# A deformable convolution block on one core: the fusion convolution with four products for two rows instead of six, and the bilinear blends made in the gather slots

## The chip, the cores and the metric

The kernel runs on one core of one Trainium2 chip. The metric is the device time of one execution in microseconds (us), the median of three timed runs. One more execution was profiled, and all rows below come from it.

## The reference, cut to what matters

```python
# x: (4, 128, 80, 80) float32; every conv is 3x3, padding 1, 128 channels out (the offsets: 18)
out_normal = conv(x, w_normal)
offset = concatenate([conv(x, w_offx), conv(x, w_offy)])     # 9 taps x (dy, dx) for each pixel
out_x = deform_conv(x, offset, w_dx)                         # bilinear samples at 9 shifted positions,
out_y = deform_conv(x, offset, w_dy)                         # then a product over channels and taps
out = conv(concatenate([out_normal, out_x, out_y]), w_fusion)  # 384 channels in
out = relu(bn(out, bn1)); out = bn(conv(out, w_conv2), bn2)
return relu(out + x)
# sample = (1-ty)(1-tx)*g00 + (1-ty)tx*g01 + ty(1-tx)*g10 + ty*tx*g11
```

## The kernel before, in words

**Tiling.** Channels lie on the 128 partitions. The four images are cut into 40 strips (NS) of 8 rows by 80 columns, 640 pixels; a half is 320 pixels, a tile 128 pixels, so a strip has 5 tiles. A float32 operand is kept as a rounded part (`hi`, float32r) and the rest (`lo`), and each product is three matmuls: hi·hi, hi·lo, lo·hi (`three`, lines 338 to 346). ScalarE (ACT) makes `hi` by a copy, VectorE (DVE) makes `lo` by a subtraction (`low`, line 636).

**Steps.** The program runs 44 steps of nine taps, all written out in order for each engine. At step i four strips are in work: the second convolution ("C") on strip i-4, the fusion convolution ("F") on strip i-2, the normal convolution ("N") and the deformable taps on strip i, and the offset convolution ("O") for strip i+1. `SLICES` gives the groups of F, N, C and O that TensorE (PE) does before the deformable tap k; F has 27 groups of three matmuls for each half. In the first four steps the order is that of `FIRST_SLICES`.

**One tap.** With T = 9i + k: GpSimd (POOL) issues five gathers for a tap, one for each tile, that bring 4 neighbours x 128 channels for 128 pixels into one of 15 slots of `cells` (line 299). ACT scales the upper two neighbours into `mixed` (`upper`), DVE adds the lower two (`sample`, line 677), ACT scales the left half into `samp` (`left`), DVE adds the right half (line 683). PE turns the five tiles (`turn_samples`, line 372), ACT and DVE make `samp_hi` and `samp_lo` from PSUM, and PE multiplies them (`deform_tap`, 12 matmuls into four banks `acc`). A slot is free for the gather 15 later when its `mixed` is done; a gather is also held back by `pace`, which PE counts up.

**Order on the engines.** Each engine works strictly through its own list. In step i, tap k the lists are: DVE `sample(T+2)`, `samples_low(T+1)`, weights, `indices`, then what ends in this tap of F, N and C; ACT `left(T+2)`, `samples_high(T+1)`, weights, `upper(T+3)`, the evacuations of O, F, N, C; PE `turn_samples(T+1)`, the slices, `deform_tap(T)`. At the end of a strip ACT copies the four `acc` halves to `feat` and DVE makes their `lo`. `feat` holds hi and lo of three groups of 128 channels, ten rows of which the first and last come from the neighbour strips (`top_done`, `bot_done`). SyncE (SP) loads x, the weights and the residual and stores the output.

Of the kernel before, what the change touches and what calls it, by code (L numbers as in the profile page):

```python
# [7 lines left out]
F32 = mybir.dt.float32  # L8
# [58 lines left out]
]  # L67
GROUPS = {"O": 3, "F": 27, "N": 9, "C": 9}

FIRST_SLICES = [  # L70
    [("O", 0, 0, 3), ("O", 1, 0, 3)],
    [("F", 0, 0, 7)],
    [("F", 0, 7, 16)],
    [("F", 0, 16, 25)],
    [("F", 0, 25, 27), ("F", 1, 0, 7)],
    [("F", 1, 7, 16)],
    [("F", 1, 16, 25)],
    [("F", 1, 25, 27), ("N", 0, 0, 7)],
    [("N", 0, 7, 9), ("N", 1, 0, 9)],
]  # L80
FIRST_STEPS = 4
WEIGHTS_AT = {1: {7: 2}, 2: {1: 3}}


def done(slices):

    return [[(j, h) for j, h, a, b in s if b == GROUPS[j]] for s in slices]

# [6 lines left out]
class Flags:  # L95


    def __init__(self, i=None):
        mid = i is None
        self.strip = mid or i < NS  # L100
        self.nxt = mid or i + 1 < NS
        self.load = mid or i + 2 < NS
        self.top = mid or 1 <= i < NS
        self.bot = mid or 1 <= i <= NS
        self.fuse = mid or 2 <= i < NS + 2
        self.mtop = mid or 3 <= i < NS + 2
        self.mbot = mid or 3 <= i <= NS + 2
        self.resid = mid or 3 <= i < NS + 3
        self.second = mid or 4 <= i < NS + 4

        first = not mid and i < FIRST_STEPS
        self.slices = FIRST_SLICES if first else SLICES
        self.done = done(self.slices)
        self.turn = 2 if first else 3
        self.weights = {} if mid else WEIGHTS_AT.get(i, {})

# [9 lines left out]
def at_least(eng, sem, value):  # L126

    if isinstance(value, int) and value <= 0:
        return
    eng.wait_ge(sem, value)  # L130


def deform_block(nc, x, xflat, table, weights, bn, const, out):
    ctx = ExitStack()
    with ctx:
# [22 lines left out]
        feat = sb("feat", [128, 2, 6, SLOT_ROWS, PITCH], F32R)  # L158
        mid = sb("mid", [128, 2, 2, SLOT_ROWS, PITCH], F32R)

        late = sb("late", [128, 18 * C])
        resid = late[:, 0:2 * PIX].rearrange("p (a n) -> p a n", n=PIX)
        mid_f = late[:, 2 * PIX:3 * PIX].rearrange("p (a n) -> p a n", n=HALF)
# [12 lines left out]
        mixed = sb("mixed", [128, 2, TILES, 2 * C])  # L176
# [8 lines left out]
        acc = [bank(f"acc{n}") for n in range(4)]  # L185
# [16 lines left out]
        slot_taken = sem("slot_taken")  # L202
# [6 lines left out]
        acc_hi_done, acc_lo_done = sem("acc_hi_done"), sem("acc_lo_done")  # L209
        n_done, n_hi_done, n_lo_done = sem("n_done"), sem("n_hi_done"), sem("n_lo_done")  # L210
        top_done, bot_done = sem("top_done"), sem("bot_done")
        f_done, f_out, mid_hi_done, mid_lo_done = sem("f_done"), sem("f_out"), sem("mid_hi_done"), sem("mid_lo_done")
# [23 lines left out]
        def _(eng):  # L236
            def load_x(c):

                start = c * (ROWS * PITCH) + c // STRIPS * (CELLS - H * PITCH) + (1 + PITCH * (LEAD - 1))

                at_least(eng, x_lo_done, c)
                eng.dma_start(x_raw[:], xflat[:, bass.ds(start, SLOT)]).then_inc(x_in, 16)

            def load_weights(n):
                a, b = CHUNKS[n]
                eng.dma_start(stage(n), weights[:, a:b]).then_inc(w_in[n], 16)
# [5 lines left out]
            load_weights(1)  # L252
            load_x(1)

            def step(i, par, fl):
                if isinstance(i, int) and i == 0:
                    eng.wait_ge(samp_done, PER // 3)
                if fl.load:
                    load_x(i + 2)
                if isinstance(i, int) and i == 1:  # L260
                    eng.wait_ge(w_lo_done, 2)
                    load_weights(2)
                    eng.wait_ge(w_lo_done, 3)
                    load_weights(3)
                if fl.resid:
                    s = i - 3
                    slot = 1 - par
                    if isinstance(i, int) and s == 0:
                        eng.wait_ge(w_lo_done, 4)

                    at_least(eng, out_stored[slot], 16 * (s // 2) if isinstance(s, int) else 8 * (s - slot))
                    eng.dma_start(resid[:, slot], x[:, bass.ds(s * PIX, PIX)]).then_inc(resid_in[slot], 16)
                if fl.second:
                    s = i - 4
                    at_least(eng, out_ready, 2 * s + 2)
                    eng.dma_start(out[:, bass.ds(s * PIX, PIX)], resid[:, par]).then_inc(out_stored[par], 16)
# [9 lines left out]
        def _(eng):  # L286
            eng.memset(feat[:].bitcast(F32), 0.0).then_inc(zeroed, 1)
            eng.memset(mid[:].bitcast(F32), 0.0).then_inc(zeroed, 1)

            def gather(c, par, b):  # L290
                at_least(eng, idx_ready, c + 1)
                for q in range(PER):
                    k, j, g = q // TILES, q % TILES, q % GSLOTS
                    at_least(eng, mixed_done, PER * c + q - GSLOTS + 1)
                    at_least(eng, pace, PER * c + q - PACE_LAG + 1)
                    if not isinstance(c, int):

                        eng.sem_inc(slot_taken, 1)
# [9 lines left out]

# [7 lines left out]
        def _(eng):  # L316
            def wcol(base, n):
                return slice((base + n) * C, (base + n + 1) * C)

            def offsets(par, half):  # L320

                for n in range(9):
                    ky, (w, part) = n // 3, ((0, x_hi), (1, x_hi), (0, x_lo))[n % 3]
                    rows = slice(half * HR + ky, half * HR + ky + HR)
                    ins = eng.matmul(work[half][:, 0:HR * PITCH], w_off[:, ky, w].rearrange("p g n -> p (g n)"),  # L325
# [22 lines left out]
            def conv(job, half, a, b, par):  # L348

                for n in range(a, b):  # L350
                    g, k = n // TAPS, n % TAPS
                    rows = slice(half * HR + k // 3, half * HR + k // 3 + HR)
                    cols = slice(k % 3, k % 3 + W)
                    if job == "F":
                        hi, lo, base = feat[:, par, 2 * g, rows, cols], feat[:, par, 2 * g + 1, rows, cols], FUSE
# [7 lines left out]
                    ins = three(work[half][:, 0:HALF], wcol(base, n), hi, lo, n == 0, n == GROUPS[job] - 1, int(mark))  # L363
                if b == GROUPS[job]:
# [10 lines left out]
            def deform_tap(T, tp, k):  # L375
                at_least(eng, samp_lo_done, T + 1)
                rest = TILES - ticks[0]
                for d, base in enumerate((DEFX, DEFY)):
                    for half in range(2):
                        n = 2 * d + half  # L380
                        px = slice(half * HALF, (half + 1) * HALF)
                        ins = three(acc[n][:, 0:HALF], wcol(base, k), samp_hi[:, tp, px], samp_lo[:, tp, px],
# [10 lines left out]
            eng.wait_ge(w_lo_done, 2)  # L393
# [450 lines left out]
```

## Time and profile before

| | us |
|---|---|
| median of 3 runs (2705.27 to 2708.77) | 2706.47 |
| the profiled execution | 2705.52 |
| its span | 2703.7 |

| engine | busy us | share | instructions |
|---|---|---|---|
| PE | 2606.2 | 96% | 17840 |
| DVE | 1845.7 | 68% | 4940 |
| ACT | 2001.4 | 74% | 4925 |
| POOL | 1881.7 | 70% | 1806 |

The granted TensorE clock was 0.984 over the span. Busy time of PE overlaps from one matmul to the next, so its distance from start to start says more than its mean duration. An engine's busy time leaves out the issue of its next instruction: POOL shows 70%, and between two gathers there is always some idle time. A duration in a timeline row with "x5" is that of five instructions from the first start to the last end. Idle time in square brackets stands before the instruction, with what ended it.

### The profile page before, as it was taken

How to read it: one execution, taken by the hardware profiler on the slowest of the kernel's cores; microseconds unless marked ns; L12 is line 12 of the kernel's file. 1: busy time of each engine (PE TensorE's matmuls, PEld its weight loads, DVE VectorE, ACT ScalarE, POOL GpSimd, SP SyncE). 2: the span in 40 equal slices, each digit the busy share in tenths (PEclk: the TensorE clock that was granted, in tenths of full speed). 3: DMA queues.
4: the chain of work that ended last, by engine and by line, in shares of the span. 5: the costliest groups of instructions: out<-in, count | busy, mean ns of one | idle time of the engine just before them, and what ended most of it. 6: DMA issues, size and time to landing. Idle time of an engine off the chain costs nothing.

```text
span 2703.7 us, 51420 instructions
## 1 busy us (share of the span) xinstructions
PE 2606.2 (96%) x17840; PEld 2598.1 (96%) x17840; DVE 1845.7 (68%) x4940; ACT 2001.4 (74%) x4925; POOL 1881.7 (70%) x1806
## 2 busy tenths in 40 slices
PE   3679999999999999999999999999999999999999
PEld 3679999999999999999999999999999999999999
DVE  5777776766676777777767776776766776777730
ACT  5678787777777777777777777777777777777741
POOL 6777777767777676777777776777767777676720
PEclk7789999999999999999999999999999999999999
DMA  5766766767666676666666666666666666666620
GB/s 170 219 203 198 213 205 205 205 189 209 197 205 199 201 206 205 200 200 204 199 203 200 203 198 201 200 200 197 200 194 206 200 205 200 203 207 195 194 76 20
DMA packets 162404, 522.70 MB, mean 193 GB/s; under 512 B 30944, under 2 KB 31072, under 8 KB 161760
## 3 DMA queue, kind: packets, MB, share of 16 engines
q0 software_dynamic: 144000, 471.97, 59.9%
q1 hardware_dynamic: 18144, 47.44, 5.1%
q8 instruction: 141, 2.31, 0.3%
q14 instruction: 119, 0.97, 0.1%
HBM read 506.18 MB, written 13.11 MB: 192 GB/s over the span
## 4 chain that ended last, share of the span: by engine, by line
PE 91%; DVE 2%; ACT 2%; DMA 2%; issue 1%; POOL 1%; ACTq 0%; POOLq 0%; DVEq 0%
PE work L340 19%; PE work L346 19%; PE work L343 19%; PE acc L343 7%; PE acc L340 7%; PE acc L346 7%; PE turned L372 7%; PE work L325 4%; DMA cells<-in_cells,index 2%; POOL cells L299 1%; DVE mixed L677 1%; ACT mixed L472 1%; PE work L332 1%; ACT samp L472 1%; DVE samp L683 0%
## 5 line engine op out<-in xcount | busy, mean ns | idle before, releaser
L299 POOL DMA_INDIRECT cells<-in_cells,index x1800 | 1870.4, 1039 | 705.1 <-issue 342.2
L472 ACT ACTIVATE mixed<-cells,wgt 128x256 f32<-128x256 f32 x1800 | 761.4, 499 | 51.2 <-DMA cells<-in_cells,index 50.4
L472 ACT ACTIVATE samp<-mixed,wgt 128x128 f32<-128x128 f32 x1800 | 620.5, 395 | 205.8 <-DVE mixed L677 197.2
L677 DVE SCALAR_TENSOR_TENSOR mixed<-cells,wgt,mixed 128x256 f32<-128x256 f32 x1800 | 745.9, 477 | 35.0 <-ACT mixed L472 33.4
L340 PE MATMUL work<-feat,w_hi 128*128 128x320 f32 x2160 | 691.4, 320 | 1.4 <-ACT off_c L471 1.4
L346 PE MATMUL work<-feat,w_lo 128*128 128x320 f32 x2160 | 676.0, 313 | 0.0
L343 PE MATMUL work<-feat,w_hi 128*128 128x320 f32 x2160 | 675.7, 313 | 0.0
L683 DVE SCALAR_TENSOR_TENSOR samp<-mixed,wgt,samp 128x128 f32<-128x128 f32 x1800 | 512.5, 345 | 59.5 <-ACT samp L472 59.5
L636 DVE TENSOR_TENSOR samp_lo<-turned,samp_hi 128x640 fp32r<-128x640 f32 x360 | 294.5, 818 | 273.8 <-ACT samp_hi L471 273.8
L340 PE MATMUL acc<-samp_hi,w_hi 128*128 128x320 f32 x1440 | 448.8, 312 | 0.0
L343 PE MATMUL acc<-samp_lo,w_hi 128*128 128x320 f32 x1440 | 447.6, 311 | 0.0
L346 PE MATMUL acc<-samp_hi,w_lo 128*128 128x320 f32 x1440 | 447.5, 311 | 0.0
L471 ACT ACTIVATE samp_hi<-turned 128x640 fp32r<-128x640 f32 x360 | 249.8, 694 | 248.2 <-PE turned L372 247.1
L340 PEld LDWEIGHTS work<-feat,w_hi 128*128 128x128 f32 x2160 | 408.4, 189 | 1.9 <-issue 1.9
L343 PEld LDWEIGHTS work<-feat,w_hi 128*128 128x128 f32 x2160 | 408.5, 189 | 0.0
L346 PEld LDWEIGHTS work<-feat,w_lo 128*128 128x128 f32 x2160 | 408.1, 189 | 0.0
L372 PE MATMUL turned<-cst,samp 128*128 128x128 f32 x1800 | 260.7, 276 | 70.0 <-DVE samp_lo L636 49.1
L372 PEld LDWEIGHTS turned<-cst,samp 128*128 128x128 f32 x1800 | 221.4, 143 | 76.0 <-issue 49.0
L340 PEld LDWEIGHTS acc<-samp_hi,w_hi 128*128 128x128 f32 x1440 | 273.9, 190 | 0.0
L343 PEld LDWEIGHTS acc<-samp_lo,w_hi 128*128 128x128 f32 x1440 | 273.3, 190 | 0.0
L346 PEld LDWEIGHTS acc<-samp_hi,w_lo 128*128 128x128 f32 x1440 | 273.1, 190 | 0.0
L340 PE MATMUL work<-mid,w_hi 128*128 128x320 f32 x720 | 230.9, 321 | 1.6 <-issue 1.6
(70 smaller groups left out, 3180.7 us busy)
## 6 DMA issues: line engine op xcount, KB each, us to landing
cells<-in_cells,index POOLq DMA_INDIRECT x1800, 3.7
x_raw<-in_xflat SPq DMA_DIRECT2D x40, 410.0 KB, 4.2
late<-in_x SPq DMA_DIRECT2D x40, 320.0 KB, 5.3
out<-late SPq DMA_DIRECT2D x40, 320.0 KB, 3.7
late<-in_weights SPq DMA_DIRECT2D x3, 1152.0 KB, 7.4
cells<-in_weights SPq DMA_DIRECT2D x1, 657.0 KB, 4.0
cst<-in_const SPq DMA_DIRECT2D x1, 199.0 KB, 4.6
bnp<-in_bn SPq DMA_DIRECT2D x1, 4.0 KB, 4.9
```

Of the source, the lines that this page charges most:

```text
L299: eng.indirect_dma_start(out=cells[:, g, :], out_offset=None, in_=table[0:(b + 1) * CELLS, :], in_offset=bass.IndirectOffsetOnAxis(ap=inde ...
L325: ins = eng.matmul(work[half][:, 0:HR * PITCH], w_off[:, ky, w].rearrange("p g n -> p (g n)"), part[:, par, rows, :], start=(n == 0), stop ...
L332: ins = eng.transpose(work[1][:, j * 96:(j + 1) * 96], off_c[:, j * 128:(j + 1) * 128], ident[0:96, 0:96])
L340: ins = eng.matmul(dst, taps_hi[:, w], hi, start=start, stop=False, skip_group_check=True)
L343: ins = eng.matmul(dst, taps_hi[:, w], lo, start=False, stop=False, skip_group_check=True)
L346: return eng.matmul(dst, w_lo[:, w], hi, start=False, stop=stop, skip_group_check=True)
L372: ins = eng.transpose(turned[:, j * 128:(j + 1) * 128], samp[:, tp, j, :], ident)
L471: return eng.activation(dst, src, ACT.Copy)
L472: return eng.activation(dst, src, ACT.Copy, scale=scale)
L636: return eng.tensor_tensor(dst, src, hi.bitcast(F32), ALU.subtract)
L677: eng.scalar_tensor_tensor(out=mixed[:, tp, j], in0=cells[:, (k * TILES + j) % GSLOTS, 2 * C:4 * C], scalar=wgt[:, par, 1, 0, j, k:k + 1], ...
L683: eng.scalar_tensor_tensor(out=samp[:, tp, j], in0=mixed[:, tp, j, C:2 * C], scalar=wgt[:, par, 1, 1, j, k:k + 1], in1=samp[:, tp, j], op0 ...
```

## The change

The fusion convolution takes its rows in pairs. For two output rows the old kernel made six row products (two rows, three weight rows); the new one makes four: with input rows r0 to r3 and weight rows w0, w1, w2 they are (r1+r2)·(w0+w1+w2)/2, (r2-r1)·(w0-w1+w2)/2, (r0-r2)·w0 and (r1-r3)·w2. `part_add` on DVE makes one of the four row sums for 3 groups x 4 row pairs x 80 columns (128x960), `part_high` on ACT and `part_low` on DVE split it in hi and lo, and PE does 9 groups of three matmuls (128x320) for each of the four. ACT copies the first product out, DVE combines it with the other three, and ACT does batch norm and relu on the whole strip at once. `feat` holds plain float32, so the splits of `acc` and N into hi and lo go. The four weight sums are made on the chip in steps 0 and 1 by DVE and ACT. The blends are written back into the gather slot: `mixed` is gone, and a slot is free only when its `samp` is done. The `acc` banks become two tensors of two banks, copied in two instructions. The slice order is new and the same in all steps. The descriptor scratch of the gathers goes from its default to 8192.

```diff
+PART_AT = {0: 0, 1: 1, 2: 2, 4: 3}
+PART_SLOTS = 3
+WEIGHTS_AT = {0: {2: 3, 5: 4}, 1: {2: 5, 5: 6}}
+SLICES = [
+    [("C", 0, 0, 9)],
+    [("O", 0, 0, 3), ("O", 1, 0, 3), ("C", 1, 0, 3)],
+    [("C", 1, 3, 9)],
+    [("F", 0, 0, 9)], [("F", 1, 0, 9)], [("F", 2, 0, 9)], [("F", 3, 0, 9)],
+    [("N", 0, 0, 9)], [("N", 1, 0, 9)],
+]
 # gpsimd
-                    at_least(eng, mixed_done, PER * c + q - GSLOTS + 1)
+                    at_least(eng, samp_done, PER * c + q - GSLOTS + 1)
 # tensor: conv, job "F"
-                        hi, lo, base = feat[:, par, 2 * g, rows, cols], feat[:, par, 2 * g + 1, rows, cols], FUSE
+                        slot = (PARTS * s + part) % PART_SLOTS
+                        hi, lo = part_hi[:, slot, n // 3, :, cols], part_lo[:, slot, n // 3, :, cols]
+                        base = FUSE + 9 * part
 # tensor: step, after the slices of tap k
+                    if k == TURN and fl.nxt:
+                        eng.wait_ge(o_out, 2 * (i + 1) + 2)
+                        turn_offsets()
 # scalar
+            def part_high(s, part):
+                q = PARTS * s + part
+                at_least(eng, part_summed, q + 1)
+                at_least(eng, f_done, q - PART_SLOTS + 1)
+                copy(part_hi[:, q % PART_SLOTS, :, :, 1:1 + W], part_sum[:]...).then_inc(part_hi_done, 1)
 # scalar: step, in the order of the list
                     left(T + 2, ...); samples_high(T + 1, 1 - tp); weights_high; upper(T + 3, ...)
+                    if fl.fuse and k in PART_AT:
+                        part_high(s, PART_AT[k])
+                    if fl.second and k in (0, 2):
+                        at_least(eng, c_out, 2 * (i - 4) + half + 1)
+                        eng.activation(part, part, ACT.Relu, bias=scale1[:, 3:4]).then_inc(out_ready, 1)
+                    if k == 1 and fl.nxt:
+                        off_evac(i + 1, 0)
+                        off_evac(i + 1, 1)
+                    if k == TURN and fl.nxt:
                         turned_evac(i + 1)
+                    if k == 3 and fl.fuse:
+                        copy(fused[:, 0:HALF], work[BANK["F", 0]][:, 0:HALF]).then_inc(prod1_out, 1)
+                    if k == 5 and fl.mtop: ...          # mid, row 0
+                    if k == 6 and fl.fuse:
+                        at_least(eng, pre_done, 2 * s + 2)
+                        eng.activation(fused[..., 640], fused[..., 640], ACT.Relu, ...).then_inc(f_out, 1)
+                        at_least(eng, f_out, s + 1)
+                        copy(mid[:, par, 0, 1:1 + ROWS, 1:1 + W], fused[..., 640]).then_inc(mid_hi_done, 1)
+                    if k == 7 and fl.mbot: ...          # mid, row 9
+                    if k in (7, 8) and fl.strip: ...    # k == 7: feat, row 0; then N: work -> feat (n_out)
+                    if k == 8 and fl.load:
+                        x_high(i + 2, par)
 # vector
+            def part_add(s, part):
+                ...waits for acc_out, n_out, top_done or bot_done, part_hi_done and part_lo_done of the part before
+                eng.tensor_tensor(part_sum[:]..., rows[:, :, first:first + 7:2, 1:1 + W],
+                                  rows[:, :, other:other + 7:2, 1:1 + W], op).then_inc(part_summed, 1)
+            def part_low(s, part):
+                at_least(eng, part_hi_done, q + 1)
+                low(part_lo[:, q % PART_SLOTS, ...], part_sum[:]..., part_hi[:, q % PART_SLOTS, ...])
+            def weights_sum(n): ...                     # three tensor_tensor of 128x384, each waits for the one before
 # vector: step, in the order of the list
+                    if k == INDEX_AT and fl.nxt:        # INDEX_AT = 3
+                        indices(i + 1, 1 - par)
+                    if fl.fuse and k in PART_AT:
+                        part_add(s, PART_AT[k])
+                    ...                                 # weights_sum in steps 0 and 1
                     sample(T + 2, ...); samples_low(T + 1, 1 - tp); weights_low
+                    if fl.fuse and k in PART_AT:
+                        part_low(s, PART_AT[k])
+                    if fl.second and k in (0, 2): ...   # c: work, resid -> resid (c_out)
+                    if fl.fuse and k == 4:
+                        eng.tensor_tensor(pre[:, :, 0], prod1, prod2, ALU.add)
+                        eng.tensor_tensor(pre[:, :, 1], prod1, prod2, ALU.subtract).then_inc(pre_half, 1)
+                    if fl.fuse and k == 5: ...          # pre[..0] += prod0  (pre_done)
+                    if fl.fuse and k == 6:              # pre[..1] -= prod3  (pre_done), then
+                        at_least(eng, mid_hi_done, s + 1)
+                        low(mid[:, par, 1, 1:1 + ROWS, 1:1 + W], fused[..., 640], mid[:, par, 0, ...])
+                    if k == 8 and fl.load:
+                        x_low(i + 2, par)
-    nc = bacc.Bacc("TRN2", target_bir_lowering=False, num_devices=1)
+    nc = bacc.Bacc("TRN2", target_bir_lowering=False, num_devices=1, dynamic_dma_scratch_size=8192)
```

## Rows read from the trace of the kernel before

**Rows 1.** The page: busy us and share of each engine; shares of the chain of waits.
```profile
PE 2606.2 (96%) x17840; PEld 2598.1 (96%) x17840; DVE 1845.7 (68%) x4940; ACT 2001.4 (74%) x4925; POOL 1881.7 (70%) x1806
PE 91%; DVE 2%; ACT 2%; DMA 2%; issue 1%; POOL 1%; ACTq 0%; POOLq 0%; DVEq 0%
```
**Rows 2.** Stretches: start:end and length; busy us by engine (instructions); clock; DMA share; GB/s.
```profile
49.80:168.60 118.80, 76.59 (x439) 74.06 (x438) 84.63 (x223) 84.86 (x211) 92.59 (x87) 0.81 0.71 213
1330.90:1395.40 64.50, 64.50 (x449) 64.44 (x448) 45.72 (x124) 49.73 (x123) 46.86 (x47) 1.00 0.69 207
2616.60:2703.70 87.10, 81.67 (x543) 81.16 (x541) 8.07 (x16) 13.43 (x27) 0.00 (x0) 1.00 0.07 23
```
**Rows 3.** Waits over the span, waiter <- releaser: us in total, times, longest us.
```profile
DVE samp_lo L636 <- ACT samp_hi L471: 273.8, 159, 6.4
ACT samp_hi L471 <- PE turned L372: 247.1, 110, 6.6
```
**Rows 4.** Timeline of PE: start, length us, line, operation, output<-inputs, shapes, count.
```profile
1353.32 0.39 PE L340 MATMUL work<-feat,w_hi 128*128 128x320 f32 x1
...
1358.34 0.31 PE L340 MATMUL acc<-samp_hi,w_hi 128*128 128x320 f32 x1
...
1360.09 0.71 PE L372 MATMUL turned<-cst,samp 128*128 128x128 f32 x5
1360.56 0.39 PE L340 MATMUL work<-feat,w_hi 128*128 128x320 f32 x1
```
**Rows 5.** Groups of instructions: count, then busy us, mean ns of one, and idle time before.
```profile
L299 POOL DMA_INDIRECT cells<-in_cells,index x1800 | 1870.4, 1039 | 705.1 <-issue 342.2 <-DVE mixed L677 235.0 <-PE work L340 92.5
L471 ACT ACTIVATE off_c<-work 32x320 f32<-32x320 f32 x240 | 102.0, 425 | 15.2 <-PE work L325 13.3
L636 DVE TENSOR_TENSOR x_lo<-x_raw,x_hi 128x820 fp32r<-128x820 f32 x40 | 40.5, 1013 | 10.8 <-ACT x_hi L471 10.8
L471 ACT ACTIVATE mid<-late 128x320 fp32r<-128x320 f32 x80 | 37.9, 473 | 2.5
L471 ACT ACTIVATE x_hi<-x_raw 128x820 fp32r<-128x820 f32 x40 | 35.2, 881 | 0.0
```
**Rows 6.** Timeline of ACT in a tap where it waits for nothing.
```profile
1333.90 1.93 ACT L472 ACTIVATE samp<-mixed,wgt 128x128 f32<-128x128 f32 x5
1335.74 0.69 ACT L471 ACTIVATE samp_hi<-turned 128x640 fp32r<-128x640 f32 x1
1336.32 2.10 ACT L472 ACTIVATE mixed<-cells,wgt 128x256 f32<-128x256 f32 x5
1338.32 0.55 ACT L608 ACTIVATE late<-late,scale 128x320 f32<-128x320 f32 x1
```
**Rows 7.** Timeline of DVE in the same tap, up to the next.
```profile
1333.34 2.05 DVE L677 SCALAR_TENSOR_TENSOR mixed<-cells,wgt,mixed 128x256 f32<-128x256 f32 x5
1335.32 1.39 DVE L683 SCALAR_TENSOR_TENSOR samp<-mixed,wgt,samp 128x128 f32<-128x128 f32 x5
1336.63 0.81 DVE L636 TENSOR_TENSOR samp_lo<-turned,samp_hi 128x640 fp32r<-128x640 f32 x1
1337.37 0.54 DVE L775 SCALAR_TENSOR_TENSOR late<-work,scale,late 128x320 f32<-128x320 f32 x1
1337.83 2.06 DVE L677 SCALAR_TENSOR_TENSOR mixed<-cells,wgt,mixed 128x256 f32<-128x256 f32 x5
```
**Rows 8.** Timeline where the indices of the next strip are made: ACT, then DVE.
```profile
1355.76 0.38 ACT L471 ACTIVATE off_s<-work 128x270 f32<-128x270 f32 x1
...
1356.17 0.25 DVE L653 TENSOR_TENSOR off_f<-off_s 128x90 f32<-128x90 f32 x1 [1.45 <-ACT off_s L471]
...
1359.44 2.07 DVE L677 SCALAR_TENSOR_TENSOR mixed<-cells,wgt,mixed 128x256 f32<-128x256 f32 x5
```
**Rows 9.** The page, DMA issues: median us from issue to landing, last.
```profile
cells<-in_cells,index POOLq DMA_INDIRECT x1800, 3.7
```
**Rows 10.** Timeline of POOL, two gathers.
```profile
136.94 0.95 POOL L299 DMA_INDIRECT cells<-in_cells,index  x1 [0.31 <-issue]
138.19 3.25 POOL L299 DMA_INDIRECT cells<-in_cells,index  x1 [0.30 <-DVE mixed L677]
```

More of the change, by code:

```diff
@@ L95, with __init__ @@
 class Flags:
[L98 to L115, printed above, removed]
+    def __init__(self, i):
+        self.strip = i < NS
+        self.nxt = i + 1 < NS
+        self.load = i + 2 < NS
+        self.top = 1 <= i < NS
+        self.bot = 1 <= i <= NS
+        self.fuse = 2 <= i < NS + 2
+        self.mtop = 3 <= i < NS + 2
+        self.mbot = 3 <= i <= NS + 2
+        self.resid = 3 <= i < NS + 3
+        self.second = 4 <= i < NS + 4
+        self.weights = WEIGHTS_AT.get(i, {})
     def has(self, job):
@@ L267, in step @@
                     slot = 1 - par
[L268 to L272, printed above, removed]
+                    if s == 0:
+                        eng.wait_ge(w_lo_done, 7)
+                    at_least(eng, out_stored[slot], 16 * (s // 2))
+                    eng.dma_start(resid[:, slot], x[:, s * PIX:(s + 1) * PIX]).then_inc(resid_in[slot], 16)
                 if fl.second:
@@ L318, in wcol, with take @@
                 return slice((base + n) * C, (base + n + 1) * C)
+            freed = [None, None]
+            def take(b):
+                if freed[b] is not None:
+                    eng.wait_ge(*freed[b])
             def offsets(par, half):
+                dst = work[BANK["O", half]]
                 for n in range(9):
@@ new lines, in step @@
+                    if k == 7 and fl.mbot:
+                        at_least(eng, mid_lo_done, min(s + 1, NS))
+                        at_least(eng, c_done, 2 * (s - 3) + 2)
+                        copy(mid[:, 1 - par, :, SLOT_ROWS - 1, 1:1 + W], mid[:, par, :, 1, 1:1 + W].bitcast(F32),
+                             scale=strip_const(s - 1, 3)).then_inc(mbot_done, 1)
+                    if k in (7, 8) and fl.strip:
+                        half = k - 7
+                        rows = slice(1 + half * HR, 1 + half * HR + HR)
+                        at_least(eng, part_summed, PARTS * (i - 2) + PARTS)
+                        if half == 0 and fl.top:
+                            at_least(eng, acc_out, 2 * i)
+                            at_least(eng, n_out, 2 * i)
+                            copy(feat[:, par, :, 0, 1:1 + W], feat[:, 1 - par, :, ROWS, 1:1 + W],
+                                 scale=strip_const(i, 2)).then_inc(top_done, 1)
+                        at_least(eng, n_done, 2 * i + half + 1)
+                        copy(feat[:, par, 0, rows, 1:1 + W],
+                             work[BANK["N", half]][:, 0:HALF].rearrange("p (r w) -> p r w", w=W)).then_inc(n_out, 1)
@@ new lines, in step @@
+                    if fl.second and k in (0, 2):
+                        half = k // 2
+                        at_least(eng, c_done, 2 * (i - 4) + half + 1)
+                        if half == 0:
+                            at_least(eng, resid_in[par], 16 * ((i - 4) // 2) + 16)
+                        part = resid[:, par, half * HALF:(half + 1) * HALF]
+                        eng.scalar_tensor_tensor(out=part, in0=work[BANK["C", half]][:, 0:HALF], scalar=scale1[:, 2:3],
+                                                 in1=part, op0=ALU.mult, op1=ALU.add).then_inc(c_out, 1)
```

437 lines of the change are left out of this document (214 added, 223 removed), and 8 rows, old and new, of the table SLICES.

## The prediction

> **What bounds the kernel now.** I read the page's busy shares and chain first, then the engines in stretches cut at strip boundaries, then the waits, then timelines. PE is busy 96% of the span and 91% of the chain of waits is PE [rows 1]. A strip ends with its last `acc` matmul; from the fifth strip to the one before last these ends lie 64.4 to 64.5 us apart, and in such a stretch PE is busy 64.50 of 64.50 us at clock 1.00, while DVE is busy 45.7 and ACT 49.7 [rows 2]. DVE waits for ACT's `samp_hi` and ACT for PE's turned tiles [rows 3]: the side engines wait for PE. The first two strips have no fusion work. There PE is busy 76.6 of 118.8 us, and POOL ran 87 gathers with 92.59 us busy [rows 2]; with the 0.30 us that always stands before the next gather [rows 10] that is 92.6 + 87 x 0.30 = 118.7 us. So POOL was full there, at 60 us a strip.
>
> **What leaves PE.** Before, F is 2 halves x 27 groups x 3 = 162 matmuls a strip; after, 4 x 9 x 3 = 108. 33 F matmuls took 1353.32 to 1358.34, or 0.150 us each allowing for the first, and 12 `acc` matmuls took 1.75 us [rows 4]. 54 fewer save 8.1 us a strip: PE needs 64.5 - 8.1 = 56.4 us. Only by this the time would fall by 40 x 8.1 = 324 us. The Trainium skill ("TensorE: Matmul & The Clock Gate", section "Wait — 56ns, not 53.3ns?") gives 2.4 GHz columns plus about 2.5 ns a matmul, by which 320 columns are an estimated 136 ns and the saving 7.3 us; the rows have 150 ns, so the trace does not quite agree.
>
> **Prices of what is added.** No row is 960 elements wide; I carry on from 820. ACT: `x_hi` (820) 0.881, `mid` (320) 0.473 [rows 5], so 0.82 ns an element and 1.00 us for `part_high`. Bounds 0.88 (no more than 820) and 1.42 (3 x 0.473). DVE: `x_lo` (820) 1.013 [rows 5], `samp_lo` (640) 0.81 [rows 7], so 1.16 us for `part_add` or `part_low`, of which the last 0.07 lies beside the next instruction: 1.09. Bounds 1.0 and 1.5. A strip gets 4 of each. DVE's load rises by about 4 x 2 x 1.09 + 4 x 0.42 (product sums of 320) less 6 `lo` parts, to some 54 us; ACT's by 4 x 1.00 and one copy less the halved row copies, to some 53. Each sum is below 56.4. Read as loads, nothing exceeds PE. But the two engines hand work to each other inside each tap, so I follow the order.
>
> **The plain tap.** Let m be the start of DVE's first `mixed`. ACT's `left` starts at m+0.56, `samp_hi` at m+2.40, `upper` at m+2.98, the next instruction at m+4.98 [rows 6, 7]. DVE starts `samp_lo` at m+3.29 and is free at m+4.03 [rows 7].
>
> **The tap with a part** (k = 0, 1, 2, 4). ACT's `part_high` stands behind `upper` in its list: m+4.98 to m+5.98. DVE's `part_low` waits for it, from m+6.01 to m+7.10, so DVE stands idle 2.0 us; behind it in DVE's list are the next tap's `part_add` (1.09) and `mixed`. ACT cannot go on either: its next `left` needs that `mixed`. From `mixed` to `mixed` that is 8.19 us instead of 4.03 to 4.5, and POOL, PE and the slots don't enter.
>
> **One strip, tap by tap** (distance to the next `mixed`):
> k=0: 7.10, then the residual sum of C 0.46 (1337.37 to 1337.83 [rows 7]), `part_add` 1.09: 8.65.
> k=1: 8.19; ACT's six `off_c` copies (0.425 each [rows 5]) run to m+8.5, before the `left` at m+8.75.
> k=2: `part_low` to 7.10, C's sum to about 7.64; ACT waits for it, relu 0.46, and only then takes `off_s` 0.38 (to 8.51) that the indices need; the index chain from its first instruction to `mixed` is 1359.44 - 1356.17 = 3.27 [rows 8]: 11.81.
> k=3: DVE free at 4.03, `part_add` 1.09: 5.12; ACT's extra copy is hidden.
> k=4: 7.10 and two sums of 0.42: 7.94.
> k=5: 4.03 + 0.42 = 4.45.
> k=6: DVE's last sum is ready when ACT is free at 4.98; relu of 640 by 0.82 (0.55 at 320 [rows 6] and 320 x 0.82 ns), to 5.80; copy 0.73, to 6.56; `low` 0.75: 7.34. DVE idles 2.1 us.
> k=7: 4.03 for DVE, but ACT has three small copies more (to 6.05).
> k=8: ACT starts `left` 6.05 - 4.03 = 2.02 after m, so `upper` ends at 6.08; N 0.35, `x_hi` 0.85 (to 7.3), DVE `x_lo` 0.95 and the next `part_add` 1.09: 9.38. ACT's two `acc` copies of 640 (0.6 each) and the row copy end at 8.9, under it.
> Sum 66.9 us a strip, against 64.5: 2.4 slower, though PE has 10 us to spare.
>
> **Does anything else come late?** PE can start tap T when the `samp` of T+1 is done, m+3.4 of the tap before. It needs 0.5 + 27 x 0.150 + 1.75 = 6.3 us, so each product of F ends by m+3.5 of the tap that uses it, and is used at m+4.0 or later; the last one (k=6) has 0.5 us to spare. PE idles some 5 us in k=3, and may show clock 0.5 (1.2 GHz) for a moment behind it, as the first two strips have 0.81 on the mean with waits of up to 6 us [rows 2, 3]. At the lower level PE could lose 2 us, once a strip, mostly into slack: 0 to +2, I take 0. Gathers: their slots are now freed 1.9 us later (`samp` 0.34 after 1335.32 against `mixed` 0.48 after 1333.34 [rows 7]). First slot free at m+2.3, four more gathers at 1.34 us, landing 3.7 after the last issue [rows 9]: m+11.4, wanted two taps on at m'+4.6. Two taps together are never under 7.34 + 4.03 = 11.4, so over 4 us remain; POOL's 60.4 (45 x (1.039 + 0.304) [rows 5, 10]) is below 66.9, and over the short taps 5 to 8 its lag stays 3 us under what `upper` allows. The in-place blends have the shapes of the old ones: 0. The smaller scratch: at most 15 gathers are open as before; 0, or up to 0.3 us a gather if it should hold one back. More waits ahead of `part_add`: 0 to +0.1 each, I take 0. The copies of `acc` and the rows save ACT about 1 us, already in.
>
> **The sum.** Strips 0 and 1 end at 168.6 [rows 2]; three fusion weight chunks with three dependent sums each, four highs and four lows go there, where POOL sets the pace and DVE's pairs of inputs hold it: +4 (0 to +15), 172.6. Strips 2 and 3 lack C: 66.9 - 0.46 - 1.44 = 65.0 each: 302.6. 34 x 66.9 = 2274.6. The last two have less to prepare, 65.0 and 58: 2700.2. The rest was 87.1 [rows 2]; 2 x 54 matmuls go (16.2) and the new chains of two products show with about 5: 76. Span 2776, with the 1.8 us that lie around it (2705.5 - 2703.7) 2778. The median of before is 1 us above the profiled run, so the two compare directly: +2.6%.
>
> **Rivals.** (1) The faster side: the handshake does not last as I have it, because DVE's `part_low` finds `part_high` done, and POOL sets the pace as in the first two strips: 172.6 + 38 x 60.4 + 76 + 1.8 = 2546. For it: that stretch is the only one where PE didn't bind. Against: there are no parts in it, and the lists fix `upper` before `part_high`. It decides if the four waits of 2.0 us and the 2.1 us of k=6 vanish. Partial forms lie between 2546 and 2700. (2) POOL is starved. Gathers issued beside DVE work take 0.95 or, behind `mixed` and `samp` back to back, 3.25 us [rows 10]. In the part taps DVE runs `part_low`, `part_add`, `mixed`, `samp` without a gap for 5.5 us instead of 3.4. If one gather in each of the four is held 2.3 us longer, POOL needs 60.4 + 9.2 = 69.6 a strip: 172.6 + 38 x 69.6 + 76 + 1.8 = 2895. The Trainium skill ("SBUF — State Buffer", section "Who interferes with whom") says that a DVE instruction with two SBUF inputs contends with a GpSimd instruction that reads SBUF; `samp_lo`, with one input in PSUM, is not of that kind, `part_low` is. By that rule this rival grows. Against it: most gathers beside `mixed` get through, the mean is only 1.039 against 0.95. (3) PE stays the bound at 56.4: 2705.5 - 16.2 - 38 x 8.1 = 2381. POOL's 60 us speak against it. (4) The parts' extra time falls fully into POOL's and PE's shadow, and the result is no change, near 2706.
>
> **Chances.** Forecast 0.60 (its own range 2735 to 2830, from 65.8 to 68.2 us a strip); (2) and lesser stalls on top of it 0.17; (1) and its partial forms 0.16; (3) 0.04; (4) 0.03. 0.2% (5 us) is what can be told from no change. Slower 0.77, same 0.03, faster 0.20. The range 2650 to 2860 leaves out (3), most of (1), and the far end of (2): 2 in 10.
>
> **What would show it.** PE busy near 56 of 67 us; `part_low` waiting for ACT `part_hi` about 2 us, 160 times (some 320 us in total); `mid` low waiting 2 us, 40 times; the distances of `mixed` in the part taps 8.2 to 8.7 and 11.8 for k=2; `part_high` 1.0 and `part_add` 1.16 us. Wrong, if `part_low` waits little; if POOL's idle is 0.30 throughout (then (1) or (2) by the mean of a gather); or if PE is 96% busy again.

## The result: 10.4% slower, and the profile after

| | before | after |
|---|---|---|
| median us (runs) | 2705.87 (4) | 2988.4 (4) |
| profiled execution, its span | 2705.52, 2703.7 | 2990.1, 2988.1 |
| ratio, 95% interval | | 1.1041 (1.1022 to 1.1060) |

The forecast had the sign and the main mechanism, but 2778 us: it foresaw 72 us of the loss and missed another 210. The first fence is the page's line of busy time (to compare with [rows 1]). The second has the stretches of the first two strips, of one step, and of the end (columns as in [rows 2]).

```profile
PE 2443.3 (82%) x15680; PEld 2375.4 (79%) x15680; DVE 2153.3 (72%) x5161; ACT 2165.3 (72%) x4977; POOL 2091.7 (70%) x1808
```
```profile
49.80:169.70 119.90, 79.68 (x443) 76.99 (x444) 90.77 (x237) 89.28 (x223) 93.38 (x88) 0.80 0.71 209
1322.60:1395.50 72.90, 59.28 (x393) 57.76 (x393) 53.35 (x128) 53.86 (x124) 53.07 (x46) 0.93 0.61 177
2904.30:2988.10 83.80, 70.89 (x435) 69.67 (x433) 26.53 (x33) 20.43 (x31) 0.00 (x0) 0.92 0.07 24
```

No engine is busy more than 82%. The first two strips end 3 us earlier than forecast (169.7 for 172.6) and the end takes 8 us more (83.8 for 76). The 38 strips between took 2734.6 us, 72.0 each, where 2527.6 was forecast, 66.5 each (66.9 in a full step). The miss of 207 us there is nearly all of it. The waits over the span (compare [rows 3]) and the gathers ([rows 5]):

```profile
ACT samp L467 <- DVE cells L684: 409.6, 268, 4.9
DVE part_lo L642 <- ACT part_hi L466: 329.9, 160, 11.7
PE work L357 <- ACT off_c L466: 210.9, 35, 6.5
POOL cells L309 <- PE work L357: 164.9, 116, 5.2
ACT cells L467 <- DMA cells<-in_cells,index: 120.0, 145, 6.8
```
```profile
L309 POOL DMA_INDIRECT cells<-in_cells,index x1800 | 2079.5, 1155 | 789.5 <-issue 362.9 <-DVE samp L691 194.2 <-PE work L357 164.9
```

The second line is the handshake: 160 times, 2.06 us each, as forecast (some 320 us). The third is a wait that the prediction does not have, and the fifth was 50.4 us before. The line of the gathers has 1155 ns on the mean, which was 1039. One tap with a part (k=1), first DVE and then ACT:

```profile
1336.79 2.06 DVE L684 SCALAR_TENSOR_TENSOR cells<-cells,wgt 128x256 f32<-128x256 f32 x5
1338.77 1.39 DVE L691 SCALAR_TENSOR_TENSOR samp<-cells,wgt,samp 128x128 f32<-128x128 f32 x5
1340.08 0.81 DVE L642 TENSOR_TENSOR samp_lo<-turned,samp_hi 128x640 fp32r<-128x640 f32 x1
1342.79 1.16 DVE L642 TENSOR_TENSOR part_lo<-part_sum,part_hi 128x960 fp32r<-128x960 f32 x1 [1.90 <-ACT part_hi L466]
1344.08 1.16 DVE L741 TENSOR_TENSOR part_sum<-feat 128x960 f32<-128x960 f32 x1
1345.16 2.06 DVE L684 SCALAR_TENSOR_TENSOR cells<-cells,wgt 128x256 f32<-128x256 f32 x5
```
```profile
1339.78 2.09 ACT L467 ACTIVATE cells<-cells,wgt 128x256 f32<-128x256 f32 x5
1341.77 0.99 ACT L466 ACTIVATE part_hi<-part_sum 128x960 fp32r<-128x960 f32 x1
1342.66 2.63 ACT L466 ACTIVATE off_c<-work 32x320 f32<-32x320 f32 x6
```

From blend to blend it is 8.37 us (8.19 forecast), `part_hi` 0.99 (1.00), `part_lo` 1.16 (1.16). Every tap can be read so. The table has the mean distance from DVE's first blend with the lower neighbours in a tap (the prediction's `mixed`, now `cells`) to that of the next, over 31 steps of each timeline. "Before" has another order, so only its sum compares. e1 to e12 are runs described below.

| k | 0 | 1 | 2 | 3 | 4 | 5 | 6 | 7 | 8 | sum |
|---|---|---|---|---|---|---|---|---|---|---|
| before | 4.49 | 4.87 | 5.30 | 11.54 | 6.87 | 4.03 | 6.43 | 11.63 | 9.31 | 64.5 |
| forecast | 8.65 | 8.19 | 11.81 | 5.12 | 7.94 | 4.45 | 7.34 | 4.03 | 9.38 | 66.9 |
| after | 9.04 | 8.37 | 14.20 | 5.10 | 7.89 | 4.42 | 7.70 | 4.03 | 11.72 | 72.5 |
| e1 | 9.05 | 8.37 | 12.10 | 5.10 | 7.89 | 4.42 | 7.66 | 4.03 | 11.64 | 70.3 |
| e8 | 8.62 | 8.37 | 14.36 | 5.10 | 7.89 | 4.42 | 7.66 | 4.07 | 9.25 | 69.8 |
| e2 | 6.63 | 6.38 | 14.30 | 5.10 | 5.89 | 4.87 | 9.04 | 4.03 | 9.61 | 65.9 |
| e3 | 6.63 | 6.40 | 12.46 | 5.10 | 5.89 | 4.87 | 9.09 | 4.03 | 10.12 | 64.6 |
| e12 | 6.63 | 6.39 | 11.44 | 5.56 | 5.89 | 4.43 | 9.03 | 4.03 | 10.25 | 63.7 |

Seven of nine taps are within 0.4 us of the forecast. Tap 2 has 2.4 us too much and tap 8 2.3: 4.7 of the 5.6 us missed. Tap 2 starts on PE in tap 1:

```profile
1337.18 0.31 PE L342 MATMUL work<-x_lo,w_off 128*128 128x328 f32 x1
1344.00 0.63 PE L357 MATMUL work<-mid,w_hi 128*128 128x320 f32 x1 [6.51 <-ACT off_c L466]
```
```profile
1349.57 0.70 ACT L466 ACTIVATE samp_hi<-turned 128x640 fp32r<-128x640 f32 x1 [1.91 <-PE turned L391]
```

C's second half goes to bank 1, which O's first half has just filled; PE cannot start it until ACT has copied O out, and that copy stands behind `upper` and `part_hi` in ACT's list (1342.66 above). PE's deformable tap 1 and the turned tiles of tap 2 come after, and ACT waits 1.91 us for them.

Tap 8 starts on POOL, whose rows come first, then ACT's:

```profile
1359.23 0.95 POOL L309 DMA_INDIRECT cells<-in_cells,index  x1 [0.30 <-issue]
1361.88 1.60 POOL L309 DMA_INDIRECT cells<-in_cells,index  x1 [1.71 <-DVE samp L691]
...
1392.87 0.95 POOL L309 DMA_INDIRECT cells<-in_cells,index  x1 [0.30 <-DVE samp L691]
```
```profile
1395.11 0.51 ACT L467 ACTIVATE cells<-cells,wgt 128x256 f32<-128x256 f32 x1 [0.92 <-DMA cells<-in_cells,index]
1396.54 0.51 ACT L467 ACTIVATE cells<-cells,wgt 128x256 f32<-128x256 f32 x1 [0.92 <-DMA cells<-in_cells,index]
```

From 1361.88 on POOL issues 20 gathers with only the usual 0.30 us between them, to 1393.82: 31.9 us. At the prediction's price (20 x 1.039 + 19 x 0.304) they would take 26.6. The last ones are those that ACT waits for, 1.84 us in all, in tap 8. In 30 strips from the middle of the timeline it is the same: a run of 20 gathers behind a wait for `samp`, 31.7 us long on the mean.

### The profile page after: what moved, and what is told of

It reads as the page before. It is cut to its first block and busy times, and to the rows that moved or that the text cites. A ratio compares the mean times of both kernels' runs of the same rounds, so it can differ in the third digit from the quotient of the medians.

```text
span 2988.1 us, 47657 instructions
## 1 busy us (share of the span) xinstructions
PE 2443.3 (82%) x15680; PEld 2375.4 (79%) x15680; DVE 2153.3 (72%) x5161; ACT 2165.3 (72%) x4977; POOL 2091.7 (70%) x1808
## 5 line engine op out<-in xcount | busy, mean ns | idle before, releaser
L309 POOL DMA_INDIRECT cells<-in_cells,index x1800 | 2079.5, 1155 | 789.5 <-issue 362.9
L467 ACT ACTIVATE samp<-cells,wgt 128x128 f32<-128x128 f32 x1800 | 662.0, 400 | 409.7 <-DVE cells L684 409.6
L467 ACT ACTIVATE cells<-cells,wgt 128x256 f32<-128x256 f32 x1800 | 775.3, 499 | 123.1 <-DMA cells<-in_cells,index 120.0
L684 DVE SCALAR_TENSOR_TENSOR cells<-cells,wgt 128x256 f32<-128x256 f32 x1800 | 744.9, 478 | 26.9 <-ACT cells L467 25.2
L691 DVE SCALAR_TENSOR_TENSOR samp<-cells,wgt,samp 128x128 f32<-128x128 f32 x1800 | 508.0, 346 | 25.5 <-ACT samp L467 25.4
L357 PE MATMUL work<-part_hi,w_hi 128*128 128x320 f32 x1440 | 467.0, 324 | 28.5 <-ACT off_s L466 28.5
L363 PE MATMUL work<-part_hi,w_lo 128*128 128x320 f32 x1440 | 452.4, 314 | 0.0
L360 PE MATMUL work<-part_lo,w_hi 128*128 128x320 f32 x1440 | 451.9, 314 | 0.0
L357 PE MATMUL work<-mid,w_hi 128*128 128x320 f32 x720 | 256.3, 356 | 220.0 <-ACT off_c L466 210.9
L642 DVE TENSOR_TENSOR part_lo<-part_sum,part_hi 128x960 fp32r<-128x960 f32 x160 | 185.5, 1159 | 329.9 <-ACT part_hi L466 329.9
L357 PEld LDWEIGHTS work<-part_hi,w_hi 128*128 128x128 f32 x1440 | 274.4, 191 | 37.8 <-ACT off_s L466 37.6
```

Source lines behind the costliest of these rows:

```text
L309: eng.indirect_dma_start(out=cells[:, g, :], out_offset=None, in_=table[0:(b + 1) * CELLS, :], in_offset=bass.IndirectOffsetOnAxis(ap=inde ...
L357: ins = eng.matmul(dst, taps_hi[:, w], hi, start=start, stop=False, skip_group_check=True)
L360: ins = eng.matmul(dst, taps_hi[:, w], lo, start=False, stop=False, skip_group_check=True)
L363: return eng.matmul(dst, w_lo[:, w], hi, start=False, stop=stop, skip_group_check=True)
L467: return eng.activation(dst, src, ACT.Copy, scale=scale)
L642: return eng.tensor_tensor(dst, src, hi.bitcast(F32), ALU.subtract)
```

## The experiments

All ratios are to the kernel before on the same chip. Theory A is the handshake of the prediction, in the first runs with PE's stall in tap 1 added; "Rival" is what else might be the case. In the cuts of code "..." stands for what is left out.

**e1: all of C's second half in tap 2.**
```diff
-    [("O", 0, 0, 3), ("O", 1, 0, 3), ("C", 1, 0, 3)],
-    [("C", 1, 3, 9)],
+    [("O", 0, 0, 3), ("O", 1, 0, 3)],
+    [("C", 1, 0, 9)],
```


> The changed kernel with all of C's second half in tap 2, so that PE has nothing in tap 1 behind O that needs the bank that O's first half holds. Theory A (my handshake sum, plus a PE stall in tap 1 that I overlooked: PE waits 6.5 us for ACT's off_c copies, and holds the gathers by their pace): tap 2 falls from 14.1 to about 11.8 us, PE's waits for off_c (469 us over work) to under 150, POOL's waits for PE (215 us) and ACT's waits for gathers (120 us) mostly go, about 67 to 68.5 us a strip: 2800 to 2860 us. Rival G (gathers, now 1155 ns long, set the pace at 45 x 1.459 = 65.7 us a strip plus their waits): POOL has only lost what it would have waited for its slots, 2940 to 2990 us.


2906.93 us, 1.0733 (1.0707 to 1.0759). PE's wait for `off_c` fell from 210.9 to 77.9 us and tap 2 from 14.20 to 12.10, as theory A had it; the time missed its range by 47 us, because ACT still waited 121 us for gathers and tap 8 stayed at 11.6.
```profile
PE work L357 <- ACT off_c L466: 77.9, 35, 2.3
ACT cells L467 <- DMA cells<-in_cells,index: 121.2, 147, 6.8
```

**e6: the pace count taken off the gathers.**
```diff
-                    at_least(eng, pace, PER * c + q - PACE_LAG + 1)
```


> The changed kernel without the pace count on the gathers; the slots alone hold them back. Theory A: the stall of PE in tap 1 reaches POOL only by the pace, so POOL's waits for PE (215 us) go, ACT's waits for gathers (120 us) shrink to under 60, and the excess of taps 7 and 8 goes (2.5 us a strip); tap 2 stays at 14.1: about 69.5 us a strip, 2890 to 2920 us. Rival: POOL's late gathers come from their own length and slots; then nothing changes, 2970 to 2990 us.


2975.46 us, 1.1001 (1.0981 to 1.1021): 0.4% under the changed kernel. This is the rival's case. POOL's wait moved from PE to the slots, ACT waits nearly as before, and tap 8 is 11.3 us instead of 11.7: PE's stall reaches it by the pace with 0.4 us at most.
```profile
POOL cells L308 <- DVE samp L690: 351.1, 409, 8.8
```
```profile
ACT cells L466 <- DMA cells<-in_cells,index: 108.5, 139, 6.8
```

**e8: gathers of 64 rows in the changed kernel**, the other half of the pixels left out. The slots are zeroed once at the start, and the first strip ends 5 us later for it.
```diff
-                        out=cells[:, g, :], ...
-                        in_offset=bass.IndirectOffsetOnAxis(ap=index[:, par, j, k:k + 1], axis=0),
+                        out=cells[0:64, g, :], ...
+                        in_offset=bass.IndirectOffsetOnAxis(ap=index[0:64, par, j, k:k + 1], axis=0),
```


> The changed kernel with gathers of 64 rows instead of 128 (half the pixels are left out). Theory A: the excess of tap 8 (11.7 us against 9.4 of my sum) is ACT waiting for gathers that DVE's pairs of SBUF inputs had lengthened: tap 8 falls to 9.4, tap 0 from 9.0 to 8.7, the wait of 120 us for gathers goes, tap 2 stays at 14.2: 69.5 to 70.2 us a strip, 2875 to 2905 us. Rival: the excess comes from PE or ACT, 2970 to 2990 us.


2890.76 us, 1.0688 (1.0666 to 1.0709). Tap 8 is 9.25 us (9.38 in the prediction) and tap 0 8.62 (8.65). The excess of tap 8 was late gathers: the same 20 now take 27.4 us, and ACT waits for none of them there. The run does not tell a shorter gather from data that lands sooner, 3.0 us after the issue instead of 3.8.
```profile
ACT cells L470 <- DMA cells<-in_cells,index: 33.3, 30, 6.3
```

**e2: `part_high` ahead of `upper` in ACT's list.**
```diff
+                    if fl.fuse and k in PART_AT:
+                        part_high(s, PART_AT[k])
                     if fl.strip and k < TAPS - 3: upper(...)
-                    if fl.fuse and k in PART_AT:
-                        part_high(s, PART_AT[k])
```


> The changed kernel with ACT's part_high ahead of upper in its list. Theory A: DVE's part_low no longer waits for upper; its wait for part_hi falls from 330 us to under 60, the part taps lose 2.0 us each, 8 us a strip, less what the tap-1 stall of PE keeps: 64 to 67 us a strip, 2680 to 2800 us. Rival G: the gathers' own rate holds it at 65.7 us a strip or more, with POOL's idle near 0.30 everywhere: not below 2750 us. If the handshake were not the cause at all, 2988 us.


2744.47 us, 1.0148 (1.0129 to 1.0168). The largest single step: three of the four part taps fall by 2.0 to 2.4 us, tap 2 keeps PE's stall, and the gathers shorten with it (1080 ns on the mean). DVE's waits now begin with others; `part_lo` is not among them:
```profile
DVE samp_lo L642 <- ACT samp_hi L466: 124.5, 86, 4.2
DVE x_lo L642 <- ACT x_hi L466: 101.1, 38, 3.5
DVE fused L839 <- PE work L363: 75.5, 39, 3.6
```

**e3: both edits, of e1 and of e2.**


> Both edits. Theory A alone gives, by the same tap sums, 6.67 + 6.21 + 11.35 + 5.1 + 5.96 + 4.45 + 7.34 + 4.03 + 9.38 = 60.5 us a strip, 170 + 38 x 60.5 + 84 = 2553 us. Rival G gives a floor of 65.7 us a strip, 2750 us, with every gap of POOL at 0.30 and a mean gather of 1.15 us or more. Between them the mean length of a gather decides.


2697.67 us, 0.9966 (0.9953 to 0.9979), between the two figures. Tap 6 costs 9.1 instead of 7.3: with the other taps shorter, PE's last product is the late one.
```profile
L309 POOL DMA_INDIRECT cells<-in_cells,index x1800 | 1979.7, 1100 | 600.8 <-issue 337.3 <-DVE samp L691 155.3 <-PE acc L357 48.1
```

**e7: e3 with gathers of 64 rows**, half the pixels left out (the edit of e8).


> Both edits of e3 and gathers of 64 rows instead of 128 (half the pixels are left out), so that POOL and the DMA engines are far from binding. Theory A: what e3 (2698 us, 64.6 us a strip) still has above the sum of 60.5 is half from gathers: the waits for gathers (117 us) go, tap 8 falls from 10.1 to 9.4 us and tap 2 from 12.5 to 12.0; tap 6 stays near 9.0, since DVE waits there for PE: 62 to 63.5 us a strip, 2600 to 2660 us. Rival: the taps are bound by ACT and DVE alone, 2690 us.


2648.85 us, 0.9793 (0.9774 to 0.9813), 63.2 us a strip: gathers hold 1.4 us of e3's strip. Of the 2.7 us that remain over 60.5, taps 2 and 6 hold 2.3.

**e5: two of nine groups in each fusion product**, the rest left out.
```diff
-                for n in range(a, b):
+                for n in ((0, 8) if job == "F" else range(a, b)):
```


> The changed kernel with 2 of the 9 groups of each of the four fusion products (the rest is left out): 84 matmuls a strip less, 12.6 us of PE's 56.4. Theory A: the tap sums are set by ACT, DVE and the gathers, and PE waits longer instead: 2950 to 2990 us, so that the 8.1 us a strip that the change took from PE bought nothing either. Rival P (PE's late products and its lower clock behind the stall of tap 1 hold the others up): under 2900 us.


2962.73 us, 1.0954 (1.0932 to 1.0976). 84 matmuls a strip less, 12.6 us at 0.150 each, brought 0.9%. PE waited longer, and its granted clock fell from 0.91 to 0.83. In this order PE's work is nearly without price. That the 54 matmuls which the change removes would also cost nearly nothing if put back is likely by this, but no run shows it.

**e4: blends in the slots alone**, in the kernel before.
```diff
-                    copy(mixed[:, tp, j], cells[:, g, 0:2 * C], scale=wgt[...])
+                    copy(cells[:, g, 0:2 * C], cells[:, g, 0:2 * C], scale=wgt[...])
-                    at_least(eng, mixed_done, PER * c + q - GSLOTS + 1)
+                    at_least(eng, samp_done, PER * c + q - GSLOTS + 1)
 ...                                                 # left and sample: cells in the place of mixed
```


> The kernel before with one part of the change alone: the blends are made in the gather slots, mixed is gone, and a slot is free when its samp is done, about 3 us later than before. Theory A: PE sets the pace at 64.5 us a strip and the slots have slack: 2701 to 2712 us, no change. Rival S (the later release of slots is itself part of the loss): POOL waits longer for DVE samp, ACT waits for gathers, 2720 us or more.


2704.55 us, 0.9999 (0.9989 to 1.0008). That half of the change costs nothing where PE sets the pace. Whether it costs something in the changed kernel, no run tests.

**e11: e4 plus eight DVE sums of two SBUF operands a strip, for which nobody waits.**
```diff
+            def extra():
+                eng.tensor_tensor(spare[:], w_hi[:, 1000:1960].bitcast(F32), w_lo[:, 1000:1960].bitcast(F32), ALU.add)
+                    if fl.fuse and fl.strip and k in (0, 1, 2, 4):
+                        extra()          # ahead of sample, and again behind samples_low
```


> The kernel before with the blends in the slots (which by itself changed nothing), plus eight sums of two SBUF operands, 128x960, on DVE in each strip from the third on, at the places of part_add and part_low but with nobody waiting for them. It tells what the added DVE work costs without the handshake. Theory A: DVE is busy 54 us of 64.5, PE stays the bound, the mean gather rises from 1.04 to 1.10 or more; 2705 to 2730 us. Rival G: the gathers become the bound at 1.155 us each (65.7 us a strip), 2750 us or more. If pairs of SBUF operands did not lengthen gathers, their mean stays at 1.04.


2795.17 us, 1.0340 (1.0324 to 1.0355): the case of Rival G. A gather takes 1169 ns, and 45 x (1.169 + 0.304) = 66.3 us against 66.5 measured a strip: with no handshake at all, the added sums make POOL the bound.
```profile
L300 POOL DMA_INDIRECT cells<-in_cells,index x1800 | 2104.5, 1169 | 561.9 <-issue 391.2 <-DVE samp L684 92.5 <-PE work L341 41.4
```

**e13: e11 with four copies of 240 columns for each sum.**
```diff
-                eng.tensor_tensor(spare[:], ...)
+                for n in range(4):
+                    eng.tensor_copy(spare[:, 240 * n:240 * n + 240], w_hi[:, ...].bitcast(F32))
```


> e11 with each added sum of two SBUF operands replaced by four copies of 240 columns with one SBUF operand, which keep DVE busy for about as long. Theory A (a gather waits for DVE instructions that read two SBUF operands): the mean gather falls back to 1.04 to 1.07 us and the time to 2703 to 2715 us. Rival 1 (a copy from SBUF to SBUF takes both ports and holds the gather as well, as the Trainium skill says of its fast mode, in SBUF — State Buffer, section Who interferes with whom): the mean gather stays at 1.10 to 1.17 us, 2720 to 2795 us. Rival 2 (any DVE work does it): as rival 1, and then gathers beside samp_lo, which reads one operand from PSUM, are long too.


2738.35 us, 1.0118 (1.0103 to 1.0134). The time lies in the range of the rivals, the gather, 1086 ns, in no one's: between e4's 1050 and e11's 1169. The copies kept DVE busy 279 us against the sums' 348, so copies lengthen gathers too, less than the sums. Rival 2 (any DVE work does it) falls: 114 gathers that in their first 0.9 us had mostly DVE work beside them, but none on two SBUF operands and none of the copies, took 951 ns on the mean. The strip took 65.3 us, more than the gathers' 62.6, so something besides them cost time; this stays open.
```profile
L300 POOL DMA_INDIRECT cells<-in_cells,index x1800 | 1954.8, 1086 | 656.6 <-issue 340.2 <-DVE samp L684 182.2 <-PE work L341 91.3
```

**e9, e10, e12: a better order.** e9 is e3 with these edits:
```diff
 # tensor, tap 2: ahead of the slices instead of behind them
+                    if k == TURN and fl.nxt: ... turn_offsets()
 # scalar: ahead of part_high
+                    if k == TURN and fl.nxt: turned_evac(i + 1)
 # scalar and vector: C's second sum and relu in tap 3
-                    if fl.second and k in (0, 2):
+                    if fl.second and k in (0, 3):
```


> Both edits of e3; further PE turns the offsets ahead of C in tap 2, ACT takes off_s ahead of part_high, and C's second sum and relu go to tap 3. By the tap sums: tap 2 6.5 + 3.3 = 9.8 us instead of 12.5, tap 3 5.6 instead of 5.1, the others as in e3: 62.4 us a strip, unless the gathers bind: 45 x (1.100 + 0.304) = 63.2 us with e3's mean gather. Theory A: the higher of the two, 170 + 38 x 63.2 + 84 = 2656 us (2640 to 2675). Rival: e3 is already held by the gathers alone, 2685 to 2700 us.


2673.61 us, 0.9886 (0.9871 to 0.9902), inside its range. e10 moves the last sum, relu and split of the fusion result to tap 7.


> e9, with the last product sum, relu and hi/lo of the fusion result in tap 7 and the row copy of mid in tap 8, where DVE and ACT have room and the product is ready. By the tap sums tap 6 falls from 9.1 to about 4.5 and tap 7 rises from 4.0 to 7.4: 60.7 us a strip; the gathers' floor stays 63.2 by e3's mean, and fewer pauses of DVE can make a gather longer. Theory A: the gathers bind, 2640 to 2665 us, hardly under e9. Rival: not bound by gathers, 170 + 38 x 60.7 + 84 = 2561 us.


2684.19 us, 0.9932 (0.9918 to 0.9945): 10 us more than e9, and 19 beyond its range. Tap 6 fell from 9.0 to 4.0, tap 7 rose from 4.0 to 10.0, and the mean gather rose to 1.114. e12 is e9 with `[("C", 1, 0, 5), ("C", 1, 5, 9)]` in tap 2 and the offsets turned between the two.


> e9 with PE doing five of the nine groups of C's second half before it turns the offsets in tap 2, so that it has work while ACT makes off_c. Theory A: PE's wait for off_c (142 us) falls under 60, taps 4 and 5 fall from 6.8 and 6.0 to 5.9 and 4.9 as in e3, the tap sum to 61.9 us, so that the gathers set the pace: 45 x (1.10 + 0.304) = 63.2 us a strip, 2645 to 2665 us. Rival (PE is not what holds e9): no change from 2674 us.


2664.75 us, 0.9831 (0.9813 to 0.9849): 1.7% faster than the kernel before, 10.8% less than the changed one (2664.75 / 2988.4, on another chip). PE's wait for `off_c` came down to 78 us and not under 60. All gaps of POOL are 0.3 us, and 45 x (1.103 + 0.304) = 63.3 us is 63.7 measured: this version is bound by its gathers.
```profile
POOL cells L309 <- issue: 341.6, 1121, 0.3
POOL cells L309 <- DVE samp L691: 103.0, 338, 0.3
POOL cells L309 <- PE work L357: 53.9, 177, 0.3
```

## Why the prediction was right in its sign and wrong in its size

- **What leaves PE, and that it buys nothing:** right. PE was busy 59.3 of 72.9 us in the step shown. That is more than the 56.4 of the prediction, at a granted clock of 0.93 instead of 1.00. e5 shows that still less PE work would hardly help.
- **The handshake:** right in kind and size. The wait was 2.06 us x 160, and its removal (e2) gave 244 us with what it drew after it. The split of `mid` in tap 6 waited for ACT 1.8 us, 40 times (2 forecast).
- **The tap sums:** right for seven taps of nine to 0.4 us, with the prices carried on from 820 columns.
- **"Does anything else come late?": the step that failed**, in two terms. First, PE's start of a tap was taken from the tiles alone. The prediction checked when each product of F is ready, and not what a bank waits for: C behind O in the same bank, +2.1 us a strip (e1). Second, the gathers were taken at 1.039 + 0.304 = 1.343 us as before, and their lag found "3 us under what `upper` allows". They took 1.155 + 0.304 = 1.459 us on the mean, and 1.6 where it counts: the run of 20 that ends in tap 8 took 5.4 us more than that price gives (31.9 for 26.6). The slack was gone, +2.4 us in tap 8 and +0.4 in tap 0 (e8).
  These are 4.9 of the 5.6 us that a full step is over the forecast. The rest is spread over taps 1, 2 and 6; tap 6 falls from 7.70 to 7.44 in e5, so some of it is PE's late last product, and the remainder stays open. In total the 38 strips missed by 207 us, the start by -3 and the end by 8, together the 212 us of the profiled run (2990.1 - 2778).
- **A rival for part of tap 8, untested:** the run of 20 gathers begins when a slot comes free, and since the change a slot is free only when its `samp` is done. The gather at 1361.88 waited 1.71 us for that. Had the first blend freed the slot as before (done at 1359.77), it could have followed the one at 1359.23 at 1360.48, 1.4 us sooner; over the 30 strips the mean is 1.5. So by this estimate from the rows, up to 1.5 of the 2.3 us that tap 8 is over the forecast may hang on the later release, and e8 does not tell this from the longer gathers. The prediction named the later release (1.9 us) and held it covered.
- **Rival (2), POOL starved, chance 0.17:** it had 69.6 us a strip and 2895 us. Its mechanism is real: e11 alone gives 66.5. It did not replace the handshake but came on top of it. The chances name "lesser stalls on top of it", but no time was worked out for them, and so the time lay outside the range.
- **Terms taken at nothing:** the slots' later release costs nothing in the kernel before (e4); in the changed one it is open, as said. Taking off the pace gives 0.4% (e6). The smaller descriptor scratch shows no price: with DVE idle beside it a gather took 0.945 us before and 0.946 after, with 0.305 us before the next in both.
- **Rivals (1), (3), (4):** fell. (1) comes true only with a better order: in e12 POOL sets the pace, and then at 63 us a strip, not 60.4.

A gather held back by DVE, POOL's rows first, then DVE's:

```profile
1340.50 0.95 POOL L309 DMA_INDIRECT cells<-in_cells,index  x1 [0.30 <-DVE samp L691]
...
1365.59 3.00 POOL L309 DMA_INDIRECT cells<-in_cells,index  x1 [0.31 <-issue]
```
```profile
1363.32 1.15 DVE L741 TENSOR_TENSOR part_sum<-feat 128x960 f32<-128x960 f32 x1
1364.38 2.07 DVE L684 SCALAR_TENSOR_TENSOR cells<-cells,wgt 128x256 f32<-128x256 f32 x5
1366.37 1.40 DVE L691 SCALAR_TENSOR_TENSOR samp<-cells,wgt,samp 128x128 f32<-128x128 f32 x5
1367.68 0.82 DVE L642 TENSOR_TENSOR samp_lo<-turned,samp_hi 128x640 fp32r<-128x640 f32 x1
```

The gather that started at 1365.59 ended at 1368.59, 0.82 us after the last `samp` (1367.77), as if its work had begun only then. Counted over the whole trace, so did nearly all that were held: of the 635 gathers of the changed kernel that took more than 1.0 us, 634 ended 0.82 us (within 0.015) after the end of a DVE instruction, and in the kernel before 484 of 485. In the changed kernel 599 gathers had practically no DVE work on two SBUF operands beside them in their first 0.9 us (under 0.05 us); they took 0.946 us on the mean, whether DVE stood idle or read an operand from PSUM. 753 had it beside them nearly all that time; they took 1.352 on the mean, though 41% of them got through in under 1.0. The one at 1340.50 is of the first kind: it began beside `samp_lo`, which reads one operand from PSUM (1340.08 to 1340.89, above), and took 0.95.

The Trainium skill ("SBUF — State Buffer", section "Who interferes with whom") says that a VectorE instruction with two SBUF inputs contends with a GpSimd instruction that reads SBUF, and one in a mode that uses both ports contends with GpSimd as well. These rows, e11's 1169 ns and e13's 1086 ns agree in direction. What part of a gather's issue is held, no run shows.

## What to carry to other kernels

When an engine's load goes down, follow every in-order list for one whole period, with the semaphores and the banks: the loads alone (53 to 56 us for DVE, ACT and PE) said 56 us and POOL's said 60, the lists said 67, and with the bank wait and the late gathers it was 72. Where one engine's result waits behind an unrelated long job of another, swap the two in that list: one moved call was worth 244 us here. An instruction's mean duration holds only for the neighbours it had; when VectorE gets more work, price the gathers anew.

## What the runs showed of the hardware that was not expected

- A gather's own time hardly depends on its rows: the median was 0.947 us with 128 rows and 0.903 with 64 (e8). The mean fell from 1155 to 1058 ns. Half the rows do not nearly halve what POOL spends on 1800 gathers.
```profile
L312 POOL DMA_INDIRECT cells<-in_cells,index x1800 | 1904.7, 1058 | 859.5 <-issue 347.0 <-PE work L360 219.3 <-DVE samp L694 216.0
```
- After the 6.51 us in which PE waited in tap 1, its matmuls of 320 columns first started 0.26 us apart instead of 0.15 (1344.44, 1344.70, 1344.97 below), the lower of the two clocks (1.2 GHz): the granted clock was 0.50 from 1337.5 to 1347.4 and 1.00 from 1347.9 on. The mean of a step was 0.91 to 0.93, and 1.00 before.
```profile
1344.44 0.47 PE L360 MATMUL work<-mid,w_hi 128*128 128x320 f32 x1
1344.70 0.47 PE L363 MATMUL work<-mid,w_lo 128*128 128x320 f32 x1
1344.97 0.47 PE L357 MATMUL work<-mid,w_hi 128*128 128x320 f32 x1
```
